# A low-rank tile in four matmuls, one expert ahead, and a quarter of the first weights' rounding on GpSimd

## The reference, cut to what matters

```
h = gelu(buf @ w1 + b1)                 # 256 -> 1024
y = h @ w2 + b2                         # 1024 -> 256
a = gelu(buf @ wd) @ wu                 # low rank: 256 -> 32 -> 256
out += (y + a)[slot of token] * weight  # for each of the two choices
sh = gelu(xt @ sw1 + sb1) @ sw2 + sb2 + gelu(xt @ swd) @ swu
out = x + out + 0.2 * sh
```

## Time and profile before

| | |
|---|---|
| median of 3 runs | 177.4 us (177.09 to 178.9) |
| the profiled execution | 177.45 us |
| its span, first to last instruction | 175.62 us |
| granted TensorE clock | 0.999 of full speed |
| busy: TensorE, VectorE, ScalarE, GpSimd | 97%, 82%, 80%, 55% |

### The profile page before, as it was taken

The page is one execution under the profiler, slowest core; times in us unless marked ns, Lnnn a source line. Parts: engine busy times, 40 slices in busy tenths (PEclk is TensorE's granted clock), DMA queues, the critical chain, the costliest instruction groups (busy, mean ns, idle before and its releaser), DMA issues.

```text
span 175.6 us, 4118 instructions
## 1 busy us (share of the span) xinstructions
PE 169.9 (97%) x1442; PEld 164.3 (94%) x1442; DVE 144.1 (82%) x330; ACT 140.5 (80%) x315; POOL 96.8 (55%) x112
## 2 busy tenths in 40 slices
PE   5799999999999999999999999999999999999994
PEld 5666879999999999999999999999999999999993
DVE  3478999998695889989889699798988989889722
ACT  3277789407888998997899799999899999897920
POOL 5835348511547572097678858868837555074700
PEclk9999999999999999999999999999999999999999
DMA  4599100069929484595987768769778598776242
GB/s 127 163 350 349 41 2 4 7 175 299 362 56 318 103 304 111 194 252 79 307 252 117 275 193 157 213 197 234 194 255 185 144 312 164 247 247 78 30 90 67
DMA packets 25981, 31.84 MB, mean 181 GB/s; under 512 B 4668, under 2 KB 22488, under 8 KB 25960
## 3 DMA queue, kind: packets, MB, share of 16 engines
q1 hardware_dynamic: 21816, 26.22, 46.7%
q0 software_dynamic: 3904, 5.25, 17.0%
q10 hardware_dynamic: 240, 0.10, 0.2%
HBM read 26.31 MB, written 5.24 MB: 180 GB/s over the span
## 4 chain that ended last, share of the span: by engine, by line
PE 93%; DMA 5%; SPq 0%; DVE 0%; issue 0%; DVEq 0%
PE y_ps L1056 14%; PE y_ps L1057 14%; PE y_ps L1058 14%; PE hid_ps L1056 10%; PE hid_ps L1057 10%; PE hid_ps L1058 10%; DMA x_in<-in_x 5%; PE turn_ps L1056 4%; PE turn_ps L1058 4%; PE turn_ps L1057 4%; PE turn_ps L1235 3%; PE row_ps L1251 1%; PE hid_ps L1095 1%; PE y_ps L1195 1%; PE y_ps L1215 1%; PE y_ps L1251 0%
## 5 line engine op out<-in xcount | busy, mean ns | idle before, releaser
L495 POOL DMA_INDIRECT out_rows<-y_row,slot_tok x23 | 38.5, 1675 | 26.8 <-DVE y_row L946 11.6
L481 POOL DMA_INDIRECT slot_in<-slot_rows,slot_src x23 | 29.5, 1281 | 17.0 <-issue 6.1
L1056 PE MATMUL y_ps<-w_h,hid_h 128*128 128x256 f32 (+2 forms) x128 | 36.4, 285 | 0.0
L1057 PE MATMUL y_ps<-w_l,hid_h 128*128 128x256 f32 (+2 forms) x128 | 36.1, 282 | 0.0
L1058 PE MATMUL y_ps<-w_h,hid_l 128*128 128x256 f32 (+2 forms) x128 | 36.1, 282 | 0.0
L741 DVE TENSOR_TENSOR hid_l<-gelu_f,hid_h 128x320 fp32r<-128x320 f32 (+3 forms) x54 | 26.5, 500 | 8.0 <-ACT hid_h L643 7.5
L1056 PE MATMUL hid_ps<-xs_h,w_h 128*128 128x248 f32 (+6 forms) x96 | 27.6, 288 | 0.0
L1058 PE MATMUL hid_ps<-xs_h,w_l 128*128 128x248 f32 (+6 forms) x96 | 27.2, 284 | 0.0
L1057 PE MATMUL hid_ps<-xs_l,w_h 128*128 128x248 f32 (+6 forms) x96 | 27.2, 284 | 0.0
L718 DVE TENSOR_TENSOR w_l<-w_raw,w_h 128x512 fp32r<-128x512 f32 x40 | 26.7, 703 | 0.0
L643 ACT ACTIVATE hid_h<-hid_ps,bias_s 128x320 fp32r<-128x320 f32 (+2 forms) x48 | 26.4, 549 | 0.0
(11 more groups left out here) (260 smaller groups left out, 465.9 us busy)
## 6 DMA issues: line engine op xcount, KB each, us to landing
w_raw<-in_L_ffn_w SPq DMA_DIRECT2D x16, 1024.0 KB
w_raw<-in_L_ffn_sw SPq DMA_DIRECT2D x3, 1024.0 KB
x_in<-in_x SPq DMA_DIRECT2D x2, 512.0 KB, 4.1
w_raw<-in_L_ffn_sw SPq DMA_DIRECT2D x2, 512.0 KB, 6.5
slot_rows<-token_row SPq DMA_DIRECT2D x8, 128.0 KB, 5.1
wu_raw<-in_L_ffn_wu SPq DMA_DIRECT2D x24, 32.0 KB
out_rows<-base SPq DMA_DIRECT2D x1, 512.0 KB
slot_in<-slot_rows,slot_src POOLq DMA_INDIRECT x23
```

The lines of the kernel that those rows point to most:

```text
L481: pool.indirect_dma_start(out=slot_in[par][0:n, s, :], out_offset=None, in_=x_rows, in_offset=bass.IndirectOffsetOnAxis(ap=slot_src[0:n, e ...
L495: pool.indirect_dma_start(out=out, out_offset=bass.IndirectOffsetOnAxis(ap=slot_tok[0:n, e, s:s + 1].bitcast(U32), axis=0), in_=y_row[0:n, ...
L1056: pe.matmul(out_ap, l_h, r_h, start=start, stop=False)
L1057: pe.matmul(out_ap, l_h, r_l, start=False, stop=False)
```

## The change

The low-rank tile takes four matmuls: the stationary operand holds the high low-rank columns twice and the low ones twice (128 columns), the moving operand is first the high and then the low part of the slots. Its upper 64 rows (high weights) and lower 64 rows (low weights) have then to be added before the gelu: ScalarE copies the lower half, VectorE adds, ScalarE runs two gelus, VectorE subtracts. The tile of expert e + 1 stands in expert e's output (ahead of f = 3 in the second half), and its steps stand among the second-weight chunks of ScalarE and VectorE. The two banks that the slots are turned into lie side by side, so that ScalarE's rounding and VectorE's subtraction of the slots are one step each. In period e GpSimd rounds chunk 3 of the first weights loaded for the next period, after the hidden tiles of expert e, and casts the low weights ahead of the gather. The counts of the hidden tiles leave out j = 0 from the first expert on.

On GpSimd:

```diff
             def period(e, par):
+                if e + 2 <= E:
+                    wd_hi_part(e + 2, par)
                 if e + 2 < E:
                     gather(e + 2, par)
-                if e + 2 <= E:
-                    wd_hi_part(e + 2, par)
+                w1_hi_part(e, par)
                 wu_hi_part(e + 2, par)
...
+            def w1_hi_part(e, par):
+                c = CHUNKS - 1
+                pool.wait_ge(hid_made, made_count(e + 2, HT - 1))
+                pool.wait_ge(w1_in, 16 * (e + 3))
+                pool.tensor_copy(w1_h[par][:, :, c * FC:H], w1_raw[:, :, c * FC:H]).then_inc(w1_hi_pool, 1)
```

On ScalarE (the last two parts in its `period`; LOW_COPY_AT is 2):

```diff
+            def low_copy(e):
+                act.wait_ge(low_made, e + 1)
+                act.activation(low_sums, halves(turn_ps[0][2 * RANK:4 * RANK, 0:SLOTS]), ACT.Copy).then_inc(low_copied, 1)
+            def low_gelu_part(e):
+                act.wait_ge(low_summed, e + 1)
+                if e > 0:
+                    act.wait_ge(low_used, e)
+                    act.wait_ge(low_split, e)
+                act.activation(low_g, low_sums[0:RANK, :, :], ACT.Gelu)
+                act.activation(halves(low_s[0:2 * RANK, 0:SLOTS]), low_sums, ACT.Gelu).then_inc(low_gelu, 1)
             def slots_hi_part(n):
-                for k in range(KD):
-                    act.activation(xs_h[:, k, 0:n], turn_ps[k][:, 0:n], ACT.Copy).then_inc(slots_hi, 1)
+                act.activation(xs_h[:, :, 0:n], turn_both[:, :, 0:n], ACT.Copy).then_inc(slots_hi, 1)
...
-                for c in range(CHUNKS):
+                for c in range(CHUNKS - 1):
                     w1_chunk(e + 2, par, c)
...
                 for c in range(CHUNKS):
+                    if c == LOW_COPY_AT and e < E - 1:
+                        low_copy(e + 1)
+                    if c == CHUNKS - 1 and e < E - 1:
+                        low_gelu_part(e + 1)
                     w2_chunk(e + 2, par, c)
```

On VectorE (the last part in its `period`):

```diff
+            def low_sum(e):
+                dve.wait_ge(low_copied, e + 1)
+                dve.tensor_tensor(low_sums, halves(turn_ps[0][0:2 * RANK, 0:SLOTS]), low_sums, ALU.add).then_inc(low_summed, 1)
+            def low_lo(e):
+                dve.wait_ge(low_gelu, e + 1)
+                dve.tensor_tensor(halves(low_s[2 * RANK:LOW, 0:SLOTS]), low_g, halves(low_s[0:RANK, 0:SLOTS].bitcast(F32)),
+                                  ALU.subtract).then_inc(low_split, 1)
...
                 for c in range(CHUNKS - LATE_LO):
+                    if c == LOW_COPY_AT - 1 and e < E - 1:
+                        low_sum(e + 1)
                     w2_chunk(c, par, e + 2)
+                if e < E - 1:
+                    low_lo(e + 1)
```

On TensorE (the second part in `expert_out`; `rows_out` does the same in its last row tile; LOW_MADE_AT is 3, and `midway` is the low tile of expert e + 1; the last part in `experts`):

```diff
+            def low_tile(e, par, size):
+                pe.wait_ge(slots_lo, e + 1)
+                pe.wait_ge(wd_lo, e + 2)
+                for k in range(KD):
+                    both = wd_s[par][:, k, :, :].rearrange("p g r -> p (g r)")
+                    pe.matmul(turn_ps[0][:, 0:size], both, xs_h[:, k, 0:size], start=(k == 0), stop=False)
+                    ins = pe.matmul(turn_ps[0][:, 0:size], both, xs_l[:, k, 0:size], start=False, stop=(k == KD - 1))
+                ins.then_inc(low_made, 1)
...
                 for f in range(NF):
+                    if m == KD - 1 and f == LOW_MADE_AT:
+                        midway()
...
                 for e, size in enumerate(sizes):
-                    pe.wait_ge(slots_lo, (e + 1) * KD)
-                    for j in range(HT):
+                    if e == 0:
+                        low_tile(0, other, size)
+                    for j in range(1, HT):
                         hidden(e + 2, j, other, e + 1, xs_h, xs_l, slice(0, size), size)
```

More of the change, by code:

```diff
@@ L84, in build @@
         y_ps = [bank(f"y_ps{i}") for i in range(2)]
-        turn_ps = [bank(f"turn_ps{i}") for i in range(2)]
+        turn_both = ctx.enter_context(nc.psum_tensor("turn_both", [P, KD, 512], F32))
+        turn_ps = [turn_both[:, k, :] for k in range(KD)]
         row_ps = bank("row_ps")
@@ L334, in held_by @@
         def held_by(u, j):
-            tiles = [i for i in range(1 if u == LAST else 0, j) if hid_banks(u)[i] is hid_banks(u)[j]]
+            tiles = [i for i in range(0 if u < 2 else 1, j) if hid_banks(u)[i] is hid_banks(u)[j]]
             return tiles[-1] if tiles else None
@@ L921, in slots_lo_part @@
                 n = MOST[e]
[L922 to L925, removed]
+                dve.wait_ge(slots_hi, e + 1)
+                dve.tensor_tensor(xs_l[:, :, 0:n], turn_both[:, :, 0:n], xs_h[:, :, 0:n].bitcast(F32),
+                                  ALU.subtract).then_inc(slots_lo, 1)
             def weigh_rows(e, par):
@@ L1001, in low_of_last, with halves @@
                 dve.memset(low_last[LOW:LOW + 2, :].bitcast(F32), 1.0).then_inc(low_last_made, 1)
+            def halves(ap):
+                return ap.rearrange("p (i n) -> p i n", i=2)
+            def low_sum(e):
[5 more added lines that the diff above has]
+                                  ALU.subtract).then_inc(low_split, 1)
             def period(e, par, rows=True):
-                for j in range(HT):
+                if e == 0:
+                    low_sum(0)
+                for j in range(1, HT):
                     split_tile(e + 2, j, MOST[e])
+                    if e == 0 and j == 1:
+                        low_lo(0)
                     if e == 0 and 1 <= j < CHUNKS - 1:
@@ L1201, in expert_out, with rows_out @@
                 ins.then_inc(y_made, 1)
-            def rows_out(e, par, size):
+            def rows_out(e, par, size, midway):
                 v = e + 1
@@ L1214, in rows_out @@
                     cols = slice(s * P, s * P + n)
-                    pe.matmul(dst, low_s[:, cols], wu_s[par][:, :], start=True, stop=False)
+                    ins = pe.matmul(dst, low_s[:, cols], wu_s[par][:, :], start=True, stop=False)
+                    if s == tiles[-1]:
+                        ins.then_inc(low_used, 1)
                     for f in range(NF):
+                        if s == tiles[-1] and f == LOW_MADE_AT:
+                            midway()
                         if s == tiles[0]:
```

70 lines of the change are left out of this document (45 added, 25 removed).

## The result

The changed kernel takes 189.83 us (median of 4 runs, 187.58 to 192.26) against 177.45 (177.09 to 178.9): ratio 1.064, 95% interval 1.052 to 1.076. The forecast was 182.2, its range ended at 185.2: the sign was right, the size was not. Ratios leave out the runs in which the chip was disturbed (among them two of the four of e3 and of e13) while the medians keep them, and the profiles of e3 and e5 are of such runs, so there the order of events is read and no time is compared.

What follows compares the result with a forecast made beforehand. TensorE's matmuls were taken as the bound. TensorE's -1.9 + 2.4 + 3.2 = +3.7, plus 2.1 for the tail's scatter, put the chain 5.8 later; last addition at 177.8, time 182.2 us, range 178.4 to 185.2.

Steps and rivals of the forecast that it cites:

- In the middle of the kernel there is just room: GpSimd in expert 3: its queue for one expert, 12.1 us, fits the 13.64 until the next expert's same point.
- the sum of 12.1: GpSimd's queue per expert: three scatters, three gathers, a pause ahead of each, the chunk and two casts, in us.
- The tail: Last experts: expert 6's scatter starts 2.1 us later, behind expert 7's hidden tiles and two casts, delaying the read-back chain.
- Rival 1: GpSimd's chunk and casts and VectorE's splits get in each other's way: 184.2 us, chance 0.15.
- Low-tile waits, 2.4: TensorE waits for the split slots at the low tiles of experts 1 to 7, 0.35 us each: +2.4.
- Turning waits, 3.2: TensorE waits for result copies before turning results: 2.0 us for expert 0, 0.4 each for experts 1 to 3.
- The saving of 1.9: TensorE's low-rank tiles: two of six matmuls removed per tile, over eight experts, saving 1.9 us.
- The single steps: The low tile's small steps on ScalarE and VectorE: 0.45 us taken, 0.35 to 0.6 kept as bounds.

Runs made afterwards that it cites:

- e3: Kernel before, with GpSimd waiting for expert e's hidden tiles ahead of the previous expert's scatter, no rounding moved: 184.3 us, ratio 1.021.
- e13: Changed kernel, GpSimd's rounding waiting only for the previous expert's hidden tiles, the last period's behind the scatter: runs 181.99, 183.45, 186.52 and 187.66 us.
- e5: Kernel before with chunk 3's rounding on GpSimd, plus one-column clears between VectorE's subtractions: 186.6 us, ratio 1.046.
- e9: Kernel before with chunk 3's rounding on GpSimd, queued behind the previous expert's scatter instead of ahead of it: 178.6 us, ratio 1.005.
- e1: Changed kernel with ScalarE rounding all four chunks again, so the low-rank part alone: 182.3 us, ratio 1.023.
- e10: Changed kernel with GpSimd's rounding queued behind the scatter: 191.1 us, ratio 1.078.
- e11: Kernel before with chunk 3's rounding on GpSimd, plus 288-column clears in three places on VectorE: 189.1 us, ratio 1.061.
- e2: Kernel before with only chunk 3's rounding moved to GpSimd, ahead of the up-weights' cast and the scatter: 185.4 us, ratio 1.045.

## Why the prediction was wrong, step by step

**The step that failed: "In the middle of the kernel there is just room".** I compared how long GpSimd's queue for one expert is (12.1) with the 13.64 between two experts. That asks whether GpSimd is busy too long, and it leaves out the time from a scatter's end on GpSimd to its landing; the deadline is another one. Expert e - 1's scatter must have landed before VectorE weighs expert e's rows, 4.4 into the next expert (102.08 - 97.67), and TensorE's output needs the bank which that weighing empties. Before, the scatter started 0.76 after its weighing. The change starts it after the hidden tiles and two casts, and in the traces each lateness is followed by the next: a late landing holds VectorE, VectorE then works without a gap, and in that stretch GpSimd's cast or scatter stands still (4.32, 4.10, 4.34 us). e3 shows that the hold costs without any added work, e9 that the work costs 0.5% without the hold; in e13's profile the changed kernel without the hold has only e1's waits. In the profile after, the four stops for weighed rows cost TensorE 4.3, counted from matmul starts as what exceeds the kernel before in the same places, and the tail 3.3. What of that is the late order by itself, what the standing still and what the slow landing is not separated: in these runs one brings on the other.

**The landing, which the sum of 12.1 leaves out.** Three of the four stops (experts 3, 4 and 7) waited for a scatter that had left GpSimd early enough. Its third transfer ended at 99.78, 116.67 and 158.28, and landed 5.4, 4.4 and 4.8 us later, with the 16 DMA engines 79 to 90% busy, the load of the next first weights among what they moved. In e9 the third transfer landed 1.7 to 2.4 after its end, with the DMA engines 43 to 77% busy. At 2.4 all three would have landed before VectorE asked (104.25, 119.54, 161.60). So the late order also moved the landings into a busier stretch; that the load slows them is likely, but no run took it apart.

**The tail** was forecast 2.1 late: 1.0 until expert 7's hidden tiles end, and two casts (0.66 + 0.40). The casts took 0.61 and 0.40; the second scatter took 4.34, not 1.7, and the rows of expert 6 themselves came late (163.11, 1.51 for a landing).

**Rival 1** named a mechanism that the traces show, with too small a price: I priced the chunk's effect on VectorE (0 to 0.3) and one cast in the tail (0.9), and left the scatters out. Its objection, that the splits wait for ScalarE with gaps between them, held only as long as VectorE wasn't late. The Trainium skill, "SBUF — State Buffer", section "Who interferes with whom", says that a VectorE instruction with two SBUF inputs contends with a GpSimd instruction that reads SBUF, and that the port pair which they share is an exclusive lock. e10 agrees that the two hold each other up, VectorE's 0.28 taking 1.04 and the cast's 0.66 taking 1.20; that one of them passes unhindered while the other waits it does not show.

**Low-tile waits, 2.4: the mechanism right, the price of a stop too low.** In e1 the brackets of experts 1 to 7 add up to 2.44. But TensorE lost 4.4 around the low tiles (some 0.5 of it at expert 0's): at 110.94, 112.01 and 112.23 in the profile after, a bracket of 0.80 is (1.07 - 0.12) + (0.22 - 0.12) = 1.05 between matmul starts, 0.25 more, 0.16 of it because the bracket starts at the end of the last matmul (0.28 long, while they start 0.12 apart). I counted waits, not stops.

**Turning waits, 3.2: too high.** Expert 0's was 1.35 of the forecast 2.0 (the sorting stood where I said, then gelus, chunk and copies in the order given); experts 1 to 3 lost some 0.5 together in place of 1.2, for which the low tile's own waits are the likely reason: they delay TensorE's asking too.

**The saving of 1.9** is consistent with e1: -1.9 + 4.4 + 2.1 (turning, with the small gaps), less 0.3 that TensorE lost at expert 0's tile before too, is 4.3, against 4.74 read at expert 7's output (160.06 - 155.32). By the forecast's terms it was 3.7. So the low-rank part was mis-sized by 1.0, GpSimd's by the rest.

**The single steps** were as estimated (0.45): the copy 0.43, the addition 0.48, the gelus 0.47 and 0.45, the low subtraction 0.48.

## What to carry to other kernels

An engine's queue has room only if each of its transfers lands before the next user of the same buffer asks, so check the deadline of what stands behind the inserted work and not the queue's length. Work put on GpSimd belongs behind its latency-bound transfers, where it cost 0.5% here and not 4.5%, and not beside VectorE's two-input subtractions on the path. Moving a tile one stage ahead spends the cover that hid its inputs' lateness; every stop that this opened cost TensorE about 0.25 us beyond the wait that the trace names.

## What the runs showed of the hardware

GpSimd's scatters, indirect transfers whose data is moved by the DMA, stood still beside VectorE's subtractions with both inputs in SBUF, as its casts did: 4.34 us (165.94, with VectorE busy without a gap until 168.85), 5.06 in e11 and 3.99 in e2, where the median of all is 1.6. In the profiles other than e3's and e5's, 19 scatters took over 2.45 us, and 18 of them ended 1.3 to 1.5 us after the end of such a stretch. But a stretch without gaps is not enough: in the tail before, the scatter at 158.23 took 1.81 beside subtractions that ran from 157.32 to 162.02 without a gap. What more it takes no run shows, so that VectorE holds the scatters is what the times suggest and not a cause that was shown.

The third transfer of an expert's scatter landed 4.4 us after its end in the middle of the changed kernel (116.67 to 121.03) but 2.2 in the tail before (160.04 to 162.22), with the DMA engines 88% and 57% busy; a load of first weights ran beside the former.
